# Last head of a two-layer cross-attention kernel: its value weights' product, its projections and its last value matmuls in another order

## The reference

```python
Q = (img_embed @ Wq).reshape(B, -1, H, D).transpose(0, 2, 1, 3)   # H = 8 heads, D = 256
K = (sent_embed @ Wk).reshape(B, -1, H, D).transpose(0, 2, 1, 3)
V = (sent_embed @ Wv).reshape(B, -1, H, D).transpose(0, 2, 1, 3)
attn = softmax(where(mask, Q @ K^T / sqrt(D), -inf))
ctx = (attn @ V).transpose(0, 2, 1, 3).reshape(B, -1, H * D)
out = ctx @ Wo + img_embed
mu, var = mean(out), var(out)                                      # over the last axis
result = (out - mu) * rsqrt(var + 1e-5) * gamma + beta
```

## Time and profile before

| what | value |
|---|---|
| median of 3 runs | 508.13 us (508.02 to 508.2) |
| the profiled execution, its own time | 507.62 us |
| span of the profiled execution | 505.8 us |
| busy: TensorE, VectorE, ScalarE, GpSimd | 475.5, 334.5, 291.4, 244.3 us |
| the last head's scores of block 2 begin | 438.46 us after the span's start |
| last matmul begins | 496.88 us |

### The profile page before, as it was taken

The page is one execution under the profiler, slowest core; times in us unless marked ns, Lnnn a source line. Parts: engine busy times, 40 slices in busy tenths (PEclk is TensorE's granted clock), DMA queues, the critical chain, the costliest instruction groups (busy, mean ns, idle before and its releaser), DMA issues.

```text
span 505.8 us, 7552 instructions
## 1 busy us (share of the span) xinstructions
PE 475.5 (94%) x2424; PEld 395.2 (78%) x2424; DVE 334.5 (66%) x681; ACT 291.4 (58%) x480; POOL 244.3 (48%) x151
## 2 busy tenths in 40 slices
PE   0989999999999999999999999999999999999992
PEld 0867787777878888888888888888888888788891
DVE  5999866566685657565856576567656765755467
ACT  4667387466665656565656665665656564656222
POOL 4636763556846362717272626363545453353004
PEclk9999999999999999999999999999999999999997
DMA  8413013758765656574747374847374745561002
GB/s 265 140 44 125 1 40 107 232 174 238 225 233 169 207 167 208 167 217 157 236 137 248 129 243 140 248 142 255 129 250 140 233 153 180 165 208 43 0 2 83
DMA packets 53974, 81.97 MB, mean 162 GB/s; under 512 B 5792, under 2 KB 43072, under 8 KB 53824
## 3 DMA queue, kind: packets, MB, share of 16 engines
q1 hardware_dynamic: 44992, 50.16, 33.7%
q10 hardware_dynamic: 8960, 31.54, 16.6%
HBM read 49.16 MB, written 32.51 MB: 161 GB/s over the span
## 4 chain that ended last, share of the span: by engine, by line
PE 82%; DVE 8%; ACT 3%; issue 2%; DMA 2%; POOL 1%; SPq 0%; DVEq 0%; ACTq 0%; POOLq 0%
PE ps_scores L611 30%; PE ps_o L634 6%; PE ps_o L635 6%; PE ps_o L638 6%; PE ps_o L637 6%; PE ps_o L636 6%; PE ps_task L561 3%; PE ps_task L560 3%; PE ps_task L559 3%; PE ps_out L559 2%; DMA ring<-in_weights_a 2%; PE ps_out L561 1%; PE ps_out L560 1%; PE ps_out L714 1%; PE ps_out L715 1%
## 5 line engine op out<-in xcount | busy, mean ns | idle before, releaser
L506 POOL TENSOR_TENSOR probs_t_lo<-probs_t_lo,probs_t_hi 128x1024 fp32r<-128x1024 f32 (+1 forms) x75 | 146.4, 1963 | 177.3 <-ACT probs_t_hi L987 177.1
L987 ACT ACTIVATE probs_t_hi<-probs_t_lo 128x1024 fp32r<-128x1024 f32 (+1 forms) x75 | 64.6, 880 | 33.8 <-DMA probs_t_lo<-scratch 33.3
L1302 DVE RECIPROCAL row_inv<-row_sum 128x1 f32<-128x1 f32 x72 | 11.4, 160 | 71.1 <-PE ps_scores L611 69.1
L634 PE MATMUL ps_o<-probs_t_hi,val_hi 128*128 128x512 f32 (+1 forms) x144 | 56.5, 393 | 1.4 <-issue 0.9
L635 PE MATMUL ps_o<-probs_t_lo,val_hi 128*128 128x512 f32 (+1 forms) x144 | 56.6, 393 | 0.0
L638 PE MATMUL ps_o<-probs_t_lo,val_rem 128*128 128x512 f32 (+1 forms) x144 | 56.4, 392 | 0.0
L637 PE MATMUL ps_o<-probs_t_hi,val_rem 128*128 128x512 f32 (+1 forms) x144 | 56.0, 389 | 0.0
L636 PE MATMUL ps_o<-probs_t_hi,val_lo 128*128 128x512 f32 (+1 forms) x144 | 55.9, 388 | 0.0
L1339 DVE STREAM_TRANSPOSE probs<-probs 128x1024 f32<-128x1024 f32 x30 | 37.3, 1245 | 24.8 <-ACT probs L975 24.8
L611 PE MATMUL ps_scores<-key_hi,q_hi 128*128 128x512 f32 x144 | 46.6, 404 | 2.2 <-DVE neg_scores L1315 1.7
L1339 DVE STREAM_TRANSPOSE neg_scores<-neg_scores 128x1024 f32<-128x1024 f32 x30 | 37.2, 1241 | 14.4 <-ACT neg_scores L975 14.4
(11 more groups left out here) (247 smaller groups left out, 1092.6 us busy)
## 6 DMA issues: line engine op xcount, KB each, us to landing
probs_t_lo<-scratch SPq DMA_DIRECT2D x240, 128.0 KB, 3.0
scratch<-neg_scores ACTq DMA_DIRECT2D x30, 512.0 KB, 3.1
scratch<-probs ACTq DMA_DIRECT2D x30, 512.0 KB, 3.8
ring<-in_weights_a SPq DMA_DIRECT2D x9, 512.0 KB, 4.9
ring<-in_weights_b SPq DMA_DIRECT2D x9, 512.0 KB, 5.7
ring<-in_keys_t SPq DMA_DIRECT2D x4, 512.0 KB, 3.4
ctx_raw<-in_context SPq DMA_DIRECT2D x2, 768.0 KB, 9.3
ring<-in_context SPq DMA_DIRECT2D x16, 96.0 KB, 2.7
```

The costliest lines, as they stand in the source:

```text
L506: nc.gpsimd.tensor_tensor(pt_lo[b][:, t, k, :], pt_lo[b][:, t, k, :].bitcast(f32), moved_part(j, k).bitcast(f32), ALU.subtract).then_inc(m ...
L634: pe.matmul(o0, val_hi[b][:, kt, :], hi, start=first, stop=False)
L987: act.activation(moved_part(j, k), pt_lo[b][:, t, k, :].bitcast(f32), ACT.Copy)\
```

## The change

For the last head alone:

- Both `absorb` products move forward on TensorE: from block 6 and from between the last value matmuls to blocks 4 and 5. Their copies (`keep_b`) move with them on ScalarE, and `split_b` moves ahead of the last `split_probs` on VectorE.
- ScalarE's `round_weights` for them moves from block 3 to block 2, where it comes ahead of `round_folded` and `exp`.
- The projections of the previous head's batch 1 run in pairs in blocks 6 and 7, in two alternating PSUM banks, with their adds; before they were one for each block from 6 on and two after the last block.
- The four projections of batch 0 come after the first four key tiles of the first half of the last value matmuls; before they came after two key tiles of the second half. The rest of the value matmuls follows in one piece.
- In the final layer norm, batch 0 is finished (statistics and centring) before the adds of batch 1; tiles 4 and 5 are centred ahead of `split_last_outputs(1)` and scaled among the last two adds; tiles 6 and 7 alone are left for the end. ScalarE scales batch 0 before its last `round_last_outputs`, and GpSimd does the additions for batch 0 ahead of `final_rstd(1)`.

```diff
 def task_no(h, j):
-    if isinstance(h, int) and h == HEADS - 1 and j >= 6:
-        return TASKS0 + 8 * h + (j - 4)
+    if isinstance(h, int) and h == HEADS - 1 and j >= QT:
+        return TASKS0 + 8 * h + (j - 2)
...
+            if isinstance(idx, int) and 8 * HEADS - QT <= idx < 8 * HEADS:
+                return (ps_out, ps_task)[idx % 2][:, 0:DIM]
...
             final_rstd(0)
-            final_rstd(1)
             for n in range(QT):
...
+            final_rstd(1)
             final_rstd(2)
...
+                elif isinstance(s, int) and 8 * HEADS - QT < s < 8 * HEADS:
+                    if s == 8 * HEADS - QT + 1:
+                        pe.wait_ge(task_free, TASKS0 + 8 * HEADS - 4)
+                    pe.wait_ge(added, s - 1)
                 elif is_last:
-                    if s == 8 * HEADS:
-                        pe.wait_ge(task_free, TASKS0 + 8 * HEADS - 4)
-
+                    if j == 2:
+                        pe.wait_ge(pt_split, 16 + 2 * QT)
...
-                    if not (last_head and (2 <= j < 6 or j == 7)):
+                    if last_head and 4 <= j < 6:
+                        if j == 4:
+                            pe.wait_ge(piece_split, pieces_b(h))
+                        pe.wait_ge(task_free, task_no(h, j))
+                        absorb(None, j - 4)
+                    elif not (last_head and j >= 2):
...
-                    if j >= 2:
+                    if last_head and j >= 6:
+                        project(h - 1, 2 * j - 8)
+                        project(h - 1, 2 * j - 7)
+                    elif j >= 2:
                         project(h - 1, j - 2)
...
             values(HEADS - 1, 0, 2)
             turn_probs(HEADS - 1, 2 * QT - 1)
-            project(HEADS - 2, 2 * QT - 2)
             values(HEADS - 1, 0, 3)
-            project(HEADS - 2, 2 * QT - 1)
-            last_values(0, range(0, 2))
-            pe.wait_ge(task_free, task_no(HEADS - 1, 7))
-            absorb(None, 1)
-            last_values(0, range(2, KT))
-            last_values(1, range(0, 2))
+            last_values(0, range(0, 4))
             for t in range(QT):
                 project(HEADS - 1, t)
-            last_values(1, range(2, 6))
+            last_values(0, range(4, KT))
+            last_values(1, range(0, 6))
...
-                    task = None if last_head and (2 <= j < 6 or j == 7) else task_no(h, j)
+                    task = None if last_head and j not in (0, 1, 4, 5) else task_no(h, j)
...
-                    if j == (3 if last_head else 4):
+                    if j == (2 if last_head else 4):
...
+                        elif last_head:
+                            if j == 4:
+                                act.wait_ge(b_split, h)
+                            keep_b(task, j - 4)
...
-            keep_b(task_no(HEADS - 1, 7), 1)
...
             round_last_outputs(0)
+            scale_finals()
             round_last_outputs(1)
-            scale_finals()
...
-                    if j >= 2:
+                    if last_head and j >= 6:
+                        add(h - 1, 2 * j - 8)
+                        add(h - 1, 2 * j - 7)
+                    elif j >= 2:
                         add(h - 1, j - 2)
...
             body(HEADS - 1)
+            dve.wait_ge(projected, 8 * HEADS)
+            dve.wait_ge(task_free, TASKS0 + 8 * (HEADS - 1) + 4)
+            split_b(HEADS)
             split_probs(HEADS - 1, 2 * QT - 1)
-            add(HEADS - 2, 2 * QT - 2)
             split_outputs(HEADS - 1, 0)
-            add(HEADS - 2, 2 * QT - 1)
...
-            final_stats(range(0, 1))
+            final_stats(range(QT))
+            final_moments(0)
             split_last_outputs(0)
-            final_stats(range(1, QT))
-            final_moments(0)
+            final_centre(range(QT))
             add(HEADS - 1, QT)
             add(HEADS - 1, QT + 1)
             final_stats(range(QT, QT + 2))
             final_moments(1)
-            final_centre(range(0, 1))
+            final_centre(range(QT, QT + 2))
             split_last_outputs(1)
-            final_centre(range(1, QT))
+            final_scale(range(QT, QT + 1))
             add(HEADS - 1, QT + 2)
+            final_scale(range(QT + 1, QT + 2))
             add(HEADS - 1, QT + 3)
             final_stats(range(QT + 2, 2 * QT))
             final_moments(2)
-            final_centre(range(QT, 2 * QT))
-            final_scale(range(QT, 2 * QT))
+            final_centre(range(QT + 2, 2 * QT))
+            final_scale(range(QT + 2, 2 * QT))
```

More of the change, by code:

```diff
@@ L1711, in final_scale @@
                         .then_inc(fin_made[1], 1)
-            dve.wait_ge(projected, 8 * HEADS)
-            dve.wait_ge(task_free, TASKS0 + 8 * (HEADS - 1) + 4)
-            split_b(HEADS)
             dve.wait_ge(added, 8 * HEADS)
```

## The result

The changed kernel takes 510.99 us (median of 14 runs, 509.15 to 512.69) beside 508.6 us for the kernel before (14 runs beside them, 507.65 to 509.56). The ratio is 1.0048, with a 95% interval of 1.0036 to 1.0059: it is 2.4 us slower. The forecast was 2.1 us slower, 510.2 us, and the result lies in its range. Runs that were slow throughout are left out of all medians and ratios: one of e11 (596.93 us) and two of the kernel before beside e5 to e8 (538.92 and 1217.6 us).

A forecast was written before the change was run, and what follows sets the result against it. TensorE, busy for 94% of the span, was taken to bound the kernel, with VectorE near the end. 4.4 us of TensorE's time less 2.3 of the tail gave +2.1 on 508.13, so 510.2 us, range 508.0 to 511.8.

The forecast's parts named there:

- part 2: Last head, blocks 2 to 7: ScalarE waits for the weights' load in block 2; last value matmuls about 4.4 us late.
- three conditions that would have made it wrong: ScalarE's wait under 3 us, TensorE's new idle time under 2.3 us, or a tail giving back more than 3.5.
- bounds that I gave the landing: Load of the weights lands 4.6 to 6.1 us after issue, moving everything by -1.2 to +0.3 us.
- wait for GpSimd's split: Block 4: TensorE ends the scores at 454.7 and waits to 455.3 for GpSimd's split before the first product.
- round trip: Block 3's spill to the rounding of what comes back: 8.5 us, possibly 8.0 or 9.5.
- clock: Rival: TensorE's clock falls to 1.2 GHz, scores and product of block 4 (3.0 us) take twice as long; 513, chance 0.03.
- delay of 4.7: First value matmuls of head 7 (block 6) come at 469.7 instead of 465.02, 4.7 us late.
- Part 1, the tail: Last adds, centrings, scalings and stores on VectorE: 2.15 us won, taken as 2.3 with the stores.
- first term: In the tail, VectorE adds as soon as the projections end instead of at 498.2: 1.6 us won.
- If TensorE came as early as now: Case for which the tail's gain was worked out: TensorE's last projections start as early as in the kernel before.
- port: VectorE's centrings of batch 0 beside GpSimd's additions: up to 0.4 us more by the skill, at most 0.3 by the row.
- the faster one (the stall does not reach the end): Rival: slack of blocks 2 to 5 absorbs ScalarE's wait, only the tail counts; 505.8 us, chance 0.11.

The follow-up runs named there:

- e11: The changed kernel timed again with no edit, beside the fillers kernel: 511.19 us, ratio 1.0054.
- e5: Changed kernel with weights rounded in block 3 and the final layer norm in the order of before; TensorE keeps the changed order: 508.69 us, ratio 1.0006.
- e8: The changed kernel timed once more with no edit: 511.94 us, ratio 1.0068.
- e1: Changed kernel with ScalarE rounding the value weights in block 3 again, all else as changed: 506.5 us, ratio 0.9961.
- e3: Changed kernel with the load of the last head's value weights issued ahead of the fetch of block 0: 506.62 us, ratio 0.9956.
- e2: Kernel before with the value weights rounded in block 2 instead of 3: 512.03 us, ratio 1.0068.
- e10: Changed kernel with 8 and 3 unused matmuls filling TensorE's waits in block 3, timed beside the changed kernel: 510.69 us, ratio 1.0044.
- e4: Changed kernel with 8 unused matmuls ahead of the projection of block 3 and 3 behind it: 510.43 us, ratio 1.0031.
- e7: Changed kernel with the folded queries ahead of the rounding of the weights, both in block 2 on ScalarE: 509.02 us, ratio 1.0017.
- e9: Kernel before with the final layer norm in the changed order on VectorE, ScalarE and GpSimd, nothing else of the change: 509.07 us, ratio 1.0015.

## Why the prediction was right, and where its terms were off

Sign, mechanism and size held: +2.1 forecast, +2.4 measured, with +3.7 and +2.8 when it was timed again. That it came so close is in part luck, since two errors, in the clock and in the other terms of part 2, pull opposite ways (below). Of the three conditions that would have made it wrong none came true: ScalarE's wait was 5.47 us (not under 3), TensorE's new idle time 1.90 + 0.67 + 0.16 us with 0.39 more at the last wait, 3.1 in all (not under 2.3), and the tail gave 2.0 (not over 3.5).

Step by step, with the 2.0 us by which this profile's last head starts later added to the forecast:

| step | forecast | measured |
|---|---|---|
| ScalarE rounds the weights | 447.75 | 447.89 |
| VectorE's split of the folded queries | 450.2 | 450.16 |
| turn of block 2 | 451.4 | 451.43 |
| idle time before the projection of block 3 | 2.1 | 1.90 |
| scores of block 4 | 454.4 | 454.62 |
| GpSimd's split of the weights | 454.8 | 454.74 |
| spill of block 3 | 457.0 | 457.06 |
| from there to the rounding of what comes back | 8.5 | 8.56 |
| first value matmuls of head 7 | 471.7 | 472.32 |
| wait before the projections of batch 0 | 0.3 to 0.5 | 0.16 |
| gain of the tail | 2.3 | 2.0 |

- **Part 2, the load.** Right, and shown by both ways of taking the wait away (e1, e3) and by the wait alone (e2). TensorE's first gap follows ScalarE's wait one for one: waits of 4.70 (e2), 5.28 (e11), 5.47 and 5.88 us (e8) gave gaps of 1.10, 1.67, 1.90 and 2.30. The bounds that I gave the landing, 4.6 to 6.1 us after the issue, were too narrow: it was 6.3 us in e8 and 6.7 in e10. Such a landing adds 0.5 to 0.9 us by the forecast's own rule.
- **The wait for GpSimd's split** (0.6 us, up to 455.3) came out smaller. In the changed kernel the slow scores covered it. At the full clock the product begins 0.55 us (e4) and 0.69 us (e10) after the last pair of score matmuls, against 0.45 in e1, so 0.1 to 0.24 us of it is left.
- **The round trip.** Its length was right, but it was not what the first value matmuls waited for: at 472.32 TensorE shows no idle time, as the slow scores had made it later than the trip. In e2 (0.20 us), e10 (0.79) and e7 the chain through the trip ended last:

```profile
468.76 0.47 PE L636 MATMUL ps_o<-probs_t_hi,val_hi 128*128 128x512 f32 x1 [0.80 <-DVE o_lo L1368]
```

  (TensorE of e7.) So the delay of 4.7 came out at 5.3 by another way than the forecast's: less waiting, more slow matmuls.
- **The clock.** This was the step most misjudged. I gave its fall a chance of 0.03, for which I took the over 3 us of idle time ahead of the drop in the earlier trace rows as the nearest row. It fell in all three profiles of the changed kernel, after shorter gaps than that. The price of 3.0 us for scores and product was high for two of them: the matmuls took 1.63 us more, since the full clock came back at the end of the scores. In e8 it stayed down for some 6.8 us, and from the scores of block 4 to the next projection it is 8.27 us against 5.37 in e1, 2.9 more. At the first value matmuls less of this is left (e8 and e11 above). The Trainium skill (TensorE: Matmul & The Clock Gate, section HAM oscillation — how this bites in real kernels) had warned that waits of TensorE throttle the work behind them, and here that warning was worth more than my row; the waits in its example are longer than those here. The result stayed in the range because the other terms of part 2 were a little too large: with the gaps filled and the clock full, e4 is 3.9 us over e1 where 4.4 was forecast, and the clock put about as much on top. That is luck and not foresight. It rests on e4; e10, the same kernel, was 2.3 us over the kernel before and e4 1.8.
- **Part 1, the tail.** 2.3 forecast, 2.0 in the profile, 2.1 by e1. The first term, the add that no longer waits for centrings, holds. The sum is worked out for the case "If TensorE came as early as now", and did not say what that rests on. e9 shows that this condition carried the whole: the order gains nothing where batch 0 is not projected earlier.
- **The port.** The forecast was 0.3 us at most from the row. The centrings of batch 0 run from 497.26 to 498.92, and GpSimd's additions begin at 498.42, half a microsecond before these end; the four took 0.41 each, as behind the adds. So the port cost nothing in this profile.

Of the rivals, the faster one (the stall does not reach the end) is refuted by e1. The gain that it would have had is real, and stands at 506.5 us once the wait is gone.

**The better versions.** e1 and e3 both beat the kernel before, by 2.1 and 2.0 us, and the changed kernel by over 4. They keep all of the change but the block in which the weights are rounded (e1), or issue the load one block earlier (e3).

## What to carry to other kernels

In an in-order stream, a wait costs by the ready work that is queued behind it: put the consumer of a load behind all work that is ready, or issue the load ahead of what holds its queue up, and compare the place with the latest landing that the trace shows, not the median. A reordering of a tail is to be judged together with what feeds it; each half alone can be worth nothing or less. And when idle time appears before dense matmuls, look at the granted clock of the windows behind it before the loss is put down to the wait alone.

## What the runs showed of the hardware

- TensorE's granted clock fell to 1.2 GHz after gaps of 1.67 us (e11) and 1.90 us (the changed kernel's first profile), each with five matmuls and a second gap of 0.67 us behind it, and in e8 after a gap of 2.30 us and the five matmuls, before the second gap had ended. It was back at 2.4 GHz after some 3.5 us in the first two and after some 6.8 us in e8, where the scores of block 4 took 4.4 us. With the gaps of e2 (1.10 and 0.67 us) and of e7 (0.22 and 0.67 us) the profiled run kept the full clock, and so it did with the gaps filled (e4) or all but 0.78 us of them (e10).
- The same load of value weights took 5.2 us from issue to landing in e3, and 5.7 (e11), 5.9 and 6.3 us (e8) in three profiles of the changed kernel; in e10 it took 6.7, beyond the spread of the earlier trace rows. The changed kernel's wait for it was 5.28 (e11), 5.47 and 5.88 us (e8).
- VectorE's centring of 128 x 256 takes 0.41 us alone, 0.77 (e5) or 0.71 (e9) beside GpSimd's additions, while its add with one input in PSUM took 0.48 beside them as well as behind them (the changed kernel, 499.87 and 504.13). The Trainium skill (SBUF — State Buffer, section Who interferes with whom) says that instructions with two SBUF inputs are the ones that collide with GpSimd; the trace agrees in kind, though the slower ones take less than twice their time and are not held for a whole addition of 0.80 us.
